# One buffer of expert rows for both expert layers, and a reordered retention with its output bias as a one-row product

## The chip, the cores and the metric

The kernel runs on one core of a Trainium2 chip. The metric is the time of one execution in device microseconds; the kernel before takes 1552.9 us, the median of three runs (1551.34 to 1556.41). The engines are TensorE (PE, with its weight loads as PEld), VectorE (DVE), ScalarE (ACT), GpSimd (POOL) and SyncE (SP, which only issues transfers).

## What is computed

The input is 4 sequences of 1024 tokens of width 256, float32. Four layers follow each other, each on the layernorm of its input and each added to it:

```
x = x + time_mix(layernorm(x))       # RWKV recurrence, projections r, k, v, output
x = x + experts(layernorm(x))        # 64 experts, 4 chosen per token, and 2 shared ones
x = x + retention(layernorm(x))      # 16 heads of 16, decay gamma, group norm, gate
x = x + experts(layernorm(x))        # the same weights again
```

The retention, cut to what matters here:

```
scores = einsum('bhnd,bhmd->bhnm', q, k) * dmask        # dmask = gamma ** (n - m)
ret    = einsum('bhnm,bhmv->bhnv', scores, v)
norm   = (ret - mean) * rsqrt(var + EPS) * gn_w + gn_b  # mean, var over a whole head of a sequence
out    = silu(x @ wg + bg) * norm @ wo + bo
```

The experts take, for each token, the four experts of highest logit plus bias, and sum their outputs with the softmax of the four logits.

## The kernel before

The 4096 tokens lie as 32 tiles of 128 in SBUF (`k.res`, 128 partitions, 32 tiles, 256 floats), where every layer adds to them. Four stages run one after the other: `time_mix`, `experts` ("moe1"), `retention`, `experts` ("moe2"). Each stage gives every engine a program of its own; engines wait for each other on semaphores, and the order of work on an engine is written out by hand.

**Experts.** In the first half tokens are routed. Each token gets four slots in a DRAM buffer of rows sorted by expert, 192 pages of 128 rows, and GpSimd scatters the normalised row to each of them (L857, 16 indirect transfers for each of 8 blocks of 4 tiles). Slots that no token takes must hold defined values, so the whole buffer is cleared before. There are two such buffers (`Slots.x`): that of moe1 has rows of 256 floats and is cleared at the end of `time_mix`'s SP program, that of moe2 has rows of 264, with a tail of 8 (the chosen experts and the numbers of the token's choices), and is cleared within the retention. Clearing is 48 transfers by `zero_slots` (L2328 to L2334), each of 512 or 528 KB. While rows are scattered, SP loads the experts' down weights over those parts of `xn` whose scatters have landed (L638, and L1091 for the last part). In the second half (`experts_*`) the pages are read in pairs (L1076), transposed (L1112), multiplied by gate and up weights (L1123), gated, multiplied by the down weights (L1136) and stored. In moe1 the stored rows are gathered only within the retention: for each tile of tokens four indirect transfers by GpSimd (L457), and VectorE adds the four with their weights (`add_pair`, L485).

**Retention** (L1490 on). Batch b is a sequence: 8 tiles, in two halves of 4. VectorE adds the choices in pairs of tiles (`add_choices(b, pair)`), takes the statistics of a half (`statistics(b, h)`), GpSimd raises the variance to the power -1/2 (`layernorm_power`, L1995), ScalarE normalises (L1889), TensorE transposes (L1714) and projects (L1730, L1735), ScalarE adds the biases and VectorE keeps the values (`keep_values`, L2133). GpSimd multiplies k and q by the decay (`decay_k`, L2004; `decay_q`, L2012), two instructions each for a half. Then the eight chunks of the batch: scores (L1777), mask on VectorE (L2143), output (L1748, L1754), update of the state (L1789; L2152, L2156). After them the group norm: sums over the group (L1798), mean, squares on ScalarE, variance (L2173), `group_power` on GpSimd (L2024), the gate on VectorE (L2181 to L2188). Then the output: four PSUM banks of two tiles, each tile two products of 128x256 (L1811), and VectorE adds each bank to `k.res` (L2211). TensorE's program for a batch is: chunks of b, first half's transposes and projections of b+1, those of the second half with the two group sums between them, output of b. `add_output_bias` (L2015 to L2020) adds the output bias to all 8 tiles of a batch on GpSimd, after ScalarE has normalised them, and VectorE's `output` waits for that.

A gather of tile t takes its place in a ring of 8 tiles and waits until the choices of tile t-8 have been added; from batch 1 on each gather also waits until the gather two before it has landed (`apart`). SP's program of the retention ends with the clearing of the second buffer: four transfers each time that another pair of tiles has been added, from the pair 4 on.

GpSimd's loop body before, for b = 0, 1, 2:

```
if b: gather(b+1, tiles 5, 6, 7)          # tiles 4 to 7 of batch 1 stand before the loop
gather(b+2, 0, 1, 2); layernorm_power(b+1, second half); gather(b+2, 3)
decay_k(b+1, first half); add_output_bias(b+1); layernorm_power(b+2, first half)
group_power(b); gather(b+2, 4); wait for the gate of b
decay_q(b+1, first); decay_k(b+1, second); decay_q(b+1, second)
```

## Time and profile before

| | |
|---|---|
| median of three runs | 1552.9 us |
| the profiled execution | 1554.35 us |
| its span, first to last instruction | 1552.7 us |
| time mixing | 0 to about 195 us |
| first expert layer | about 195 to 604 us |
| retention | about 604 to 1005 us |
| second expert layer | about 1005 us to the end |
| busy: TensorE, VectorE, GpSimd, ScalarE | 1276.3, 1110.2, 935.1, 686.9 us |
| mean granted clock of TensorE | 0.918 of full speed |
| clearing transfers | 48 of 512 KB and 48 of 528 KB, median 15.2 and 5.0 us to landing |

Times are microseconds from the start of the span. A timeline row is a run of like instructions of one engine: start, time from its start to the end of the last of them, line and operation, output and inputs, count, and in brackets the idle time of the engine before it and what ended it. A float32 product is two MATMUL instructions. Ends of matmuls are modelled, so distances between starts say more than durations. "128*128" is the part of the array that a matmul takes (rows*columns), and what follows it is the shape of its operand.

### The profile page before, as it was taken

What the parts mean: (1) busy time and instruction counts of PE and PEld (TensorE: products, weight loads), DVE (VectorE), ACT (ScalarE), POOL (GpSimd) and SP (SyncE); (2) the same over time, 40 slices, a digit from 0 to 9 for tenths busy, and PEclk for the clock granted to TensorE, in tenths of its full rate; (3) what the DMA queues carried; (4) which work ended last, traced back from release to release, by engine and by line L of the source; (5) the groups of instructions that cost most, each with busy time, mean ns of one, the idle gap of its engine ahead of it and who ended that gap; (6) DMA issues with size and microseconds to landing.
All of it is one profiled execution on the core that took longest, in us unless ns stands there. A gap on an engine that the chain in (4) does not pass through costs nothing. (4 is left out here: it accounts for less than half of the span.)

```text
span 1552.7 us, 24667 instructions
## 1 busy us (share of the span) xinstructions
PE 1276.3 (82%) x7400; PEld 872.7 (56%) x7400; DVE 1110.2 (72%) x2782; ACT 686.9 (44%) x1463; POOL 935.1 (60%) x1064
## 2 busy tenths in 40 slices
PE   6688666998799996988889899576998688888683
PEld 2244443665688884556465656453665566666442
DVE  4899888778366663538567766587776488888777
ACT  4999531221366664232415243231221477676520
POOL 2999747777555554765565522057777377777700
PEclk9799867999899997998999999868999899999987
DMA  9900073232788786432534430072323765655187
GB/s 360 419 7 0 0 294 102 100 108 93 229 257 280 261 282 217 124 138 84 218 104 163 156 122 1 8 302 105 112 102 115 213 198 193 214 185 156 41 312 258
DMA packets 115882, 257.41 MB, mean 166 GB/s; under 512 B 21895, under 2 KB 43822, under 8 KB 115252
## 3 DMA queue, kind: packets, MB, share of 16 engines
q1 hardware_dynamic: 87572, 188.32, 35.3%
q0 software_dynamic: 27648, 67.70, 12.8%
q8 instruction: 52, 0.85, 0.2%
q14 instruction: 66, 0.54, 0.1%
q10 hardware_dynamic: 544, 0.00, 0.0%
HBM read 124.56 MB, written 139.75 MB: 170 GB/s over the span
## 5 line engine op out<-in xcount | busy, mean ns | idle before, releaser
L857 POOL DMA_INDIRECT slots_x<-arena,slot x256 | 272.1, 1063 | 102.4 <-issue 74.2
L1204 POOL DMA_INDIRECT pairs_y<-arena x192 | 189.4, 986 | 79.8 <-issue 45.2
L1123 PE MATMUL moe_narrow<-arena 128*128 128x128 f32 x1536 | 209.5, 280 | 31.6 <-DVE arena L1267 31.2
L1123 PEld LDWEIGHTS moe_narrow<-arena 128*128 128x128 f32 x1536 | 188.5, 194 | 43.4 <-issue 41.6
L700 PE MATMUL moe_wide<-arena 128*128 128x512 f32 x384 | 188.2, 637 | 18.6 <-DVE arena L975 18.6
L1267 DVE TENSOR_TENSOR arena<-arena,moe_narrow 64x128 f32<-64x128 f32 x384 | 111.6, 291 | 98.7 <-ACT arena L1171 92.2
L457 POOL DMA_INDIRECT arena<-slots_y,slot x128 | 128.9, 1007 | 87.2 <-DMA arena<-slots_y,slot 51.3
L1165 ACT ACTIVATE arena<-moe_narrow 128x512 f32<-128x512 f32 x192 | 114.6, 597 | 104.6 <-PE moe_narrow L1123 57.0
L1112 PE MATMUL moe_narrow<-ident,arena 128*128 128x128 f32 x768 | 126.0, 289 | 17.3 <-DMA arena<-slots_x 17.3
L1275 DVE COPY arena<-moe_wide 128x512 f32<-128x512 f32 x192 | 128.4, 689 | 7.4 <-DMA pairs_y<-arena 2.7
L700 PEld LDWEIGHTS moe_wide<-arena 128*128 128x128 f32 x384 | 77.0, 207 | 99.5 <-issue 98.4
L485 DVE SCALAR_TENSOR_TENSOR residual<-arena,gate,residual 128x256 f32<-128x256 f32 x256 | 114.6, 519 | 24.2 <-DMA arena<-pairs_y 14.8
L1181 ACT ACTIVATE arena<-arena 64x256 f32 x288 | 118.5, 411 | 26.7 <-issue 13.6
L785 ACT ACTIVATE arena<-moe_wide 128x512 f32<-128x512 f32 x48 | 28.7, 597 | 217.0 <-PE moe_wide L700 217.0
L1136 PE MATMUL moe_wide<-arena 64*128 64x256 f32 x768 | 122.1, 415 | 3.1 <-ACT arena L1181 1.6
L1112 PEld LDWEIGHTS moe_narrow<-ident,arena 128*128 128x128 f32 x768 | 86.0, 144 | 63.9 <-issue 61.0
L1065 POOL COPY arena<-arena 128x256 f32 x192 | 70.8, 397 | 80.7 <-PE moe_narrow L1123 64.7
L711 PE MATMUL moe_narrow<-arena 128*128 128x256 f32 x384 | 92.7, 395 | 14.4 <-DVE arena L975 12.7
L1730 PE MATMUL ret_pj<-arena 128*128 128x512 f32 x192 | 91.0, 615 | 9.8 <-ACTq L1902 6.2
L711 PEld LDWEIGHTS moe_narrow<-arena 128*128 128x128 f32 x384 | 73.7, 197 | 27.1 <-DVE arena L975 14.4
L2143 DVE TENSOR_TENSOR arena<-ret_sc,arena 128x512 f32<-128x512 f32 x128 | 79.4, 682 | 10.4 <-PE ret_sc L1777 6.3
L1171 ACT ACTIVATE arena<-moe_narrow 64x256 f32<-64x256 f32 x192 | 72.1, 375 | 18.6 <-PE moe_narrow L1123 14.6
(273 smaller groups left out, 2409.1 us busy)
## 6 DMA issues: line engine op xcount, KB each, us to landing
slots_x<-arena SPq DMA_DIRECT2D x48, 528.0 KB, 5.0
arena<-slots_x SPq DMA_DIRECT2D x96, 264.0 KB, 2.9
slots_x<-arena SPq DMA_DIRECT2D x48, 512.0 KB, 15.2
arena<-slots_x SPq DMA_DIRECT2D x96, 256.0 KB, 3.6
slots_y<-arena SPq DMA_DIRECT2D x96, 256.0 KB, 3.1
arena<-w_gu SPq DMA_DIRECT2D x2, 8192.0 KB, 27.7
arena<-pairs_y SPq DMA_DIRECT2D x32, 512.0 KB, 4.7
residual<-x SPq DMA_DIRECT2D x8, 512.0 KB, 9.0
```

Of the source, the lines that this page charges most:

```text
L457: pool.indirect_dma_start(out=self.ring[:, t % self.G, i, :], in_=self.k.slots.y, out_offset=None, in_offset=bass.IndirectOffsetOnAxis(ap= ...
L485: dve.scalar_tensor_tensor(tile, self.ring[:, place + j, i, :], weight, tile, ALU.mult, ALU.add)\
L700: last = pe.matmul(bank[:, :], sgu[:, h, at:at + P], xnt[n % TRING][:, h, :], start=h == 0, stop=h == KH - 1)
L711: last = pe.matmul(down_ps[:, i, :], sht[:, (SH * n + m) % HRING, at:at + P], sd[:, m, :], start=m == 0, stop=m == SH - 1)
L857: pool.indirect_dma_start(out=x_slots, in_=xn[:, t, :], in_offset=None, out_offset=bass.IndirectOffsetOnAxis(ap=slot[:, t, i:i + 1], axis=0))\
L1112: last = pe.transpose(xt_ps[n % 2][:, (j * KH + h) * P:(j * KH + h + 1) * P], xin[:, n % XRING, j, h * P:(h + 1) * P], k.ident[:, :])
L1123: last = pe.matmul(h_ps[n % 2][:, j * P:(j + 1) * P], weights[:, n % 3, j, h, :], xt[:, n % XTRING, (j * KH + h) * P:(j * KH + h + 1) * P] ...
L1136: last = pe.matmul(y_ps[n % 2][:, j, 0:D], ht[rows, n % HTRING, j * P:(j + 1) * P], wd_pair[rows, n % HTRING, :], start=True, stop=True)
L1165: act.activation(xt[:, n % XTRING], xt_ps[n % 2][:, :], ACT.Copy).then_inc(exp_sem("xt_read"), 1)
L1181: act.activation(wd_pair[j * F:(j + 1) * F, n % HTRING, :], down_of(held[n][j]), ACT.Copy)\
L1204: pool.indirect_dma_start(out=slots.y_of, in_=ytile[:, n % YRING, j, :], in_offset=None, bounds_check=slots.pairs - 1, oob_is_err=False, o ...
L1275: dve.tensor_copy(ytile[:, n % YRING], y_ps[n % 2][:, :, 0:D]).then_inc(exp_sem("y_kept"), 1)
```

## The change

One buffer `slots_x` with rows of 264 floats serves both expert layers. It is cleared once, at the end of `time_mix`; the second clearing, in the retention, goes. In moe1 GpSimd clears the tails of the rows in SBUF with one memset, and the rows are scattered with them. In the retention the output bias becomes a third product for each tile: one row of ones (partition 0 of `one_row`) by one row of the bias, added into the bank of the output by TensorE. `add_output_bias` and its waits go. GpSimd's gathers, powers and decays stand in another order, and on VectorE the statistics of batch b+2 move behind the gate, in front of the output. The checks of the arena against `ZERO_AT` become checks against its whole size. Not shown are the signatures and the calls, which lose `zeroes` and `turn`.

```diff
@@ class Slots @@
-        self.x = [nc.dram_tensor(f"slots_x{turn}", (self.tiles * P, width + tail), F32, kind="Internal").ap()
-                  for turn, tail in ((1, 0), (2, self.TAIL))]
+        self.x = nc.dram_tensor("slots_x", (self.tiles * P, width + self.TAIL), F32, kind="Internal").ap()
@@ experts, route_gpsimd @@
             if scatters:
                 pool.iota(xn[:, :, D + K:D + 2 * K], ...)
+            else:
+                pool.memset(xn[:, :, D:W], 0.0).then_inc(sem("tables"), 1)
...
-            pool.wait_ge(k.slots_zeroed, 16 * k.ZEROINGS * (1 + scatters))
-            pool.wait_ge(sem("tables"), 2 if scatters else 1)
+            pool.wait_ge(k.slots_zeroed, 16 * k.ZEROINGS)
+            pool.wait_ge(sem("tables"), 2)
@@ retention, sync @@
-            PAIRS = NT // 2
-            for pair in range(TB // 2, PAIRS) if zeroes else ():
-                sp.wait_ge(sem("added"), 2 * choices.K * (pair + 1))
-                k.zero_slots(sp, 2, range(k.ZEROINGS * (pair - TB // 2) // (PAIRS - TB // 2),
-                                          k.ZEROINGS * (pair + 1 - TB // 2) // (PAIRS - TB // 2)))
@@ retention, tensor, output @@
                         for c in range(CH):
                             at = (2 * i + j) * P
-                            last = pe.matmul(outs[i % 2][:, j * D:(j + 1) * D], ret[:, c, at:at + P], wo[:, c, :],
-                                             start=c == 0, stop=c == CH - 1)
+                            pe.matmul(outs[i % 2][:, j * D:(j + 1) * D], ret[:, c, at:at + P], wo[:, c, :],
+                                      start=c == 0, stop=False)
+                        last = pe.matmul(outs[i % 2][:, j * D:(j + 1) * D], one_row[0:1, :], bias_o[0:1, :],
+                                         start=False, stop=True)
@@ retention, scalar, normalise @@
-                if h == H - 1:
-                    act.wait_ge(sem("xn_ready"), TB * (b + 1))
-                    act.sem_inc(sem("choices_added"), 1)
@@ retention, gpsimd @@
-            def add_output_bias(b):
...
             def constants():
...
+                pool.memset(one_row, 1.0).then_inc(sem("one_row"), 1)
...
             layernorm_power(H)
-            gather(1, [4, 5, 6, 7])
-            pool.wait_ge(sem("w_o"), 16 * LOADS)
-            add_output_bias(0)
+            gather(1, [4, 5])
             for b in range(B - 1):
                 more = b + 2 < B
-                if b:
-                    gather(b + 1, [5, 6, 7])
+                gather(b + 1, [6, 7])
                 if more:
-                    gather(b + 2, [0, 1, 2])
+                    gather(b + 2, range(4))
                 layernorm_power(H * (b + 1) + 1)
                 if more:
-                    gather(b + 2, [3])
-                decay_k(b + 1, 0)
-                add_output_bias(b + 1)
+                    gather(b + 2, [4, 5])
+                group_power(b)
+
+                pool.wait_ge(sem("gated"), CH * (b + 1))
+                for h in range(H):
+                    decay_k(b + 1, h)
+                    decay_q(b + 1, h)
                 if more:
                     layernorm_power(H * (b + 2))
-                group_power(b)
-                if more:
-                    gather(b + 2, [4])
-                pool.wait_ge(sem("gated"), CH * (b + 1))
-                decay_q(b + 1, 0)
-                decay_k(b + 1, 1)
-                decay_q(b + 1, 1)
             group_power(B - 1)
@@ retention, vector @@
             def output(b):
-                dve.wait_ge(sem("bias_added"), b + 1)
...
             keep_values(0, 0)
-            keep_values(0, 1)
             add_choices(1, 1)
             statistics(1, 0)
+            keep_values(0, 1)
...
                 if b + 2 < B:
                     add_choices(b + 2, 0)
                     add_choices(b + 2, 1)
-                    statistics(b + 2, 0)
                 variance(b)
                 gate(b)
                 keep_values(b + 1, 1)
+                if b + 2 < B:
+                    statistics(b + 2, 0)
                 output(b)
```

## Rows read from the trace of the kernel before

**Rows 1.** Busy times of one stretch: PE, PEld, DVE, ACT, POOL, clock, DMA share, GB/s

```profile
740.00:745.00 5.00, 4.60 (x11) 1.67 (x10) 3.14 (x8) 4.27 (x7) 4.57 (x2) 1.00 0.92 361
```

**Rows 2.** Timeline of DVE, batch 0: start us, busy us, instruction, idle before

```profile
688.39 0.76 DVE L2133 TENSOR_TENSOR arena<-ret_pj,arena 128x256 f32<-128x256 f32 x2 [14.06 <-PE ret_pj L1735]
...
696.83 0.27 DVE L2140 MEMSET arena<- 128x256 f32 x1 [0.55 <-DVE arena L2108]
...
725.06 4.93 DVE L2156 SCALAR_TENSOR_TENSOR arena<-arena 128x128 f32<-128x128 f32 x2
...
778.91 0.16 DVE L2181 TENSOR_TENSOR arena<-arena 128x2 f32<-128x2 f32 x1 [1.83 <-POOL arena L2024]
...
793.90 0.27 DVE L2140 MEMSET arena<- 128x256 f32 x1
```

**Rows 3.** Timeline of DVE, batches 1 and 2

```profile
862.64 0.16 DVE L2181 TENSOR_TENSOR arena<-arena 128x2 f32<-128x2 f32 x1 [1.83 <-POOL arena L2024]
...
876.73 0.27 DVE L2140 MEMSET arena<- 128x256 f32 x1
...
939.93 0.16 DVE L2181 TENSOR_TENSOR arena<-arena 128x2 f32<-128x2 f32 x1 [0.88 <-POOL arena L2024]
...
952.21 0.27 DVE L2140 MEMSET arena<- 128x256 f32 x1
```

**Rows 4.** Timeline of POOL, batches 0 to 2

```profile
698.23 1.03 POOL L457 DMA_INDIRECT arena<-slots_y,slot  x1 [0.49 <-issue]
...
726.01 3.82 POOL L2019 TENSOR_TENSOR residual<-residual,arena 128x2048 f32<-128x2048 f32 x1
...
756.12 1.22 POOL L1995 TENSOR_TENSOR arena<-arena,minus_half 128x4 f32<-128x4 f32 x1
...
788.28 2.49 POOL L2004 TENSOR_TENSOR arena<-arena 128x512 f32<-128x512 f32 x2
...
793.39 0.98 POOL L457 DMA_INDIRECT arena<-slots_y,slot  x1 [0.16 <-issue]
...
830.16 0.95 POOL L457 DMA_INDIRECT arena<-slots_y,slot  x1 [0.31 <-issue]
840.25 1.05 POOL L1995 TENSOR_TENSOR arena<-arena,minus_half 128x4 f32<-128x4 f32 x1 [9.13 <-DVEq L2110]
...
923.06 1.05 POOL L1995 TENSOR_TENSOR arena<-arena,minus_half 128x4 f32<-128x4 f32 x1 [27.44 <-DVEq L2110]
```

**Rows 5.** Timeline of PE, first output products of batches 0 to 2

```profile
783.31 3.75 PE L1811 MATMUL ret_rt<-arena 128*128 128x256 f32 x8 [4.75 <-DVE arena L2188]
...
867.03 3.75 PE L1811 MATMUL ret_rt<-arena 128*128 128x256 f32 x8 [5.69 <-DVE arena L2188]
...
944.33 1.97 PE L1811 MATMUL ret_rt<-arena 128*128 128x256 f32 x8 [0.17 <-DVE arena L2188]
946.13 1.89 PE L1811 MATMUL ret_sc<-arena 128*128 128x256 f32 x8
```

**Rows 6.** Timeline of PE in the two expert stages

```profile
418.18 1.06 PE L1123 MATMUL moe_narrow<-arena 128*128 128x128 f32 x8
419.07 0.60 PE L1112 MATMUL moe_narrow<-ident,arena 128*128 128x128 f32 x4
419.51 1.06 PE L1123 MATMUL moe_narrow<-arena 128*128 128x128 f32 x8
420.49 1.13 PE L1136 MATMUL moe_wide<-arena 64*128 64x256 f32 x8
421.56 0.66 PE L1112 MATMUL moe_narrow<-ident,arena 128*128 128x128 f32 x4
422.05 1.06 PE L1123 MATMUL moe_narrow<-arena 128*128 128x128 f32 x8
...
1228.98 0.70 PE L1136 MATMUL moe_wide<-arena 64*128 64x256 f32 x4
```

**Rows 7.** Timeline of POOL, start of the first expert stage

```profile
413.38 0.39 POOL L1226 COPY arena<-arena 64x256 f32 x1 [7.88 <-DMA arena<-w_d]
```

More of the change, by code:

```diff
@@ L1485, in _, with retention @@
                 sum_vector(dve)
-def retention(nc, k, w_qk, w_vg, w_o, b_q, b_k, b_vg, b_o, gn_w, gn_b, gamma, sw_gu, sw_d, batches, zeroes):
+def retention(nc, k, w_qk, w_vg, w_o, b_q, b_k, b_vg, b_o, gn_w, gn_b, gamma, sw_gu, sw_d, batches):
     B = batches
@@ L1526, in retention @@
     blocks = arena.take(P)
+    one_row = arena.take(P)
     stats = arena.take(BLK, 6)
@@ L2013, in decay_q @@
                         .then_inc(sem("qst_ready"), 1)
-            def add_output_bias(b):
-                pool.wait_ge(sem("choices_added"), b + 1)
-                tiles = k.res[:, bass.ds(TB * b, TB), :]
-                pool.tensor_tensor(tiles, tiles, bias_o.unsqueeze(1).to_broadcast([P, TB, D]), ALU.add)\
-                    .then_inc(sem("bias_added"), 1)
             def group_power(b):
```

15 lines of the change are left out of this document (8 added, 7 removed).

## The prediction

> **What bounds the kernel now.** The change touches three stages, so I read the trace by stage: first the timelines of the retention (604.6 to 1003.5 us of the span of 1552.7), then the start of the expert stage of the first expert layer. The retention is a loop over four batches. In its chunk part VectorE sets the pace and nothing of the change lies there, except one stall. Between the chunk parts stands a chain: layernorm power on GpSimd, ScalarE's normalisation, TensorE's transposes and projections, the group's variance, VectorE's gate, TensorE's output products, VectorE's adds, and the next chunk part, whose first VectorE instruction is the memset of L2140. Three lengths of the chain matter:
> - From power (L1995, the second half's) to the start of the gate (L2181): batch 2, where nothing else is queued, needs 923.06 to 939.93, 16.9 us. Batch 0 needs 756.12 to 778.91, 22.8, and batch 1 840.25 to 862.64, 22.4 [rows 2 to 4].
> - From the first output product (L1811) to the next L2140: 783.31 to 793.90, 10.6 us in batch 0; 867.03 to 876.73, 9.7 in batch 1; 944.33 to 952.21, 7.9 in batch 2 [rows 2, 3, 5]. The first eight matmuls are at 3.75 us in the first two and 1.97 in the third: TensorE had stood idle for 4.75 and 5.69 us before and ran at half rate, in batch 2 it had not [rows 5].
> - The power itself. In batch 1 GpSimd sat idle 9.13 us before it and waited for VectorE. In batch 0 it was still in its gathers [rows 4].
>
> **The change, part by part**, on the profiled execution (1554.35 us, 1.5 above the median of 1552.9; I apply the difference to the median).
>
> *Second clearing removed.* 48 transfers of 528 KB leave SP's queue. Nothing is queued behind them there but the end of the stage, so SP gains nothing. They shared the DMA engines with GpSimd's gathers: at 740 to 745 us the queues moved 361 GB/s, while a gather every 1.74 us of 131 KB is 75 [rows 1, 4]. The effect is in the gather rate below.
>
> *Bias off GpSimd.* Four additions of 3.82 us go. Beside the first, at 726.01, two small products of VectorE (L2156, on the chain of the chunk part) lasted 4.93 us [rows 2, 4]. That stall of at most 4.9 us is worth something only if GpSimd's gathers are not later, and they are (next), so I count nothing for it. The second addition stood in batch 1 between the power and the gate and is counted there.
>
> *GpSimd's order, batch 0.* Every instruction of the move counted: before the power of batch 0, it had 28 gathers (tiles 4 to 7 of the next batch, 0 to 2 of the one after) and a bias addition; now it has 32 (four more: tile 3) and none. The first 16 took 698.23 to 726.01, 1.74 each; the 24 of batch 1, free of clearing, 793.39 to about 831.1, 1.57 each [rows 4]. I take 1.74 for the same first 16 and 1.65, between the two, for the other 16: 27.8 + 26.4 = 54.2 us. They start about 2.0 us earlier, at 696.2, because VectorE's statistics of the next batch no longer stand behind the values of the second half: two pairs of 0.76 us and a wait between them, before which VectorE idled 14.06 us [rows 2]. The chunk part itself starts earlier by between 0 and 2 us, which the later wait for GpSimd swallows. The power comes at 750.4 instead of 756.12. Bounds: same start and 1.74 throughout gives 755.8, no gain; 1.5 throughout gives 744.
>
> *From power to gate, batches 0 and 1.* The statistics of the batch after next move from before the variance to behind the gate, and the decay of k and the bias addition, which blocked VectorE's choices, move behind the gate or go. Next late is then TensorE, which gives the 16.9 us of batch 2. For batch 1: 22.4 to 16.9, 5.5 us. For batch 0, TensorE still idles before the late normalisation, so I take 18.5 rather than 16.9: gate at 768.9 instead of 778.91, 10.0 us. Behind the power there are 8 gathers now, 13 us, before the group's power, which is needed after 16: they just fit, and if each were 0.4 us slower the group's power would be late by one or two.
>
> *Behind the gate.* TensorE's output no longer follows an idle stretch (its projections end about when the gate ends, as in batch 2), so both batches take the 7.9 us of batch 2 before the new products: 2.7 and 1.8 us less. The statistics lie beside the first two output products. The four decays (two instructions and 2.49 us each [rows 4]) run from the gate on, 10 us in all; the first is needed when the next chunk part starts, at least 7.9 us later, the second a chunk behind it. The layernorm power behind them is needed only at the third chunk. All are hidden; uncovered, the first decay would cost 2.5 us.
> Gains: batch 0, 10.0 + 2.7 = 12.7; batch 1, 5.5 + 1.8 = 7.3; together **20.0 us**. Batches 2 and 3 gain nothing.
>
> *Third products.* Two per output bank, four banks per batch, four batches: 32, all on the chain, since VectorE's add waits for each bank. A product of 256 columns is two MATMULs. Eight take 944.33 to 946.13, 1.80 us, so streaming costs 0.45 us each; rows of contraction save nothing [rows 5]. But the trace names each matmul by a part of the array: operands of 64 rows come as 64*128, and one of a single row will not come as 128*128 (inferred). What a change of part costs shows in the first layer's expert stage, where TensorE never waits. Eight L1123 among their like take 0.89 us (418.18 to 419.07), four L1112 0.44 (419.07 to 419.51). The eight 64-row L1136 cost 0.43 more busy time than four do (1.13 against 0.70), so four more cost what two of the full array would, and eight are 0.85 of work. From 419.51 to 422.05 stand eight L1123, eight L1136 and four L1112: 2.54 us, where 0.89 + 0.85 + 0.44 = 2.18 would do [rows 6]. A round trip costs **0.36 us**. Each third product stands between full ones, so each makes a round trip: 0.45 + 0.36 = 0.81 us, by 32 is 25.9; with 0.4 more for the last batch, whose output starts after an idle stretch, **26.3 us**. Bounds: 0.45 each (14.4 in all) without the round trip, 1.0 each (32.0) if it is dearer for a single row or at a lower clock.
> The Trainium skill, TensorEngine Tiling (Array Packing), Key Properties, has a rule against this change: changing the tiling mode, and not just the tile, drains TensorE. By that rule two drains stand around each third product; the trace agrees, as far as 0.36 us per round trip is one. Without it the sum would end 11.5 us lower.
>
> *Rows of 264 in the first layer.* Scatters and loads are those of the second layer now, issued at the same pace. The last load of down weights carries five experts instead of four, and GpSimd waits 7.88 us for it [rows 7]. If landing grows with bytes that is 2 us, if its start dominates nothing; I take 0.5, the low side, since a load's wait includes the rows ahead of it. The small memsets fall into idle time; the clearing of 528 instead of 512 KB ends a hundred us before it is needed.
>
> **Sum:** -20.0 + 26.3 + 0.5 = +6.8 us, 1554.35 to 1561.2 on the profiled execution, 1552.9 to **1559.7** on the median. A measurement tells about 0.3% (4.7 us) from nothing.
>
> **Rivals.**
> 1. *The third product only streams* (place: TensorE between L1811's; price 0.45). For it: TensorE could take a single row on the full array. Against it: both neighbours in rows 6. Net -20.0 + 14.8 + 0.5 = -4.7: 1548.2. It decides by the round trip's price p: net is -4.7 + 32p, so the kernel is not slower if p is under 0.15, and slower by over 0.3% only if p is over 0.29.
> 2. *The gathers run faster* once nothing shares the queues: power at 744, gate 16.9 behind it, 8 us more gain, net -1.2: 1551.7. For it: 361 GB/s at the slow gathers. Against: the first 16 were slow with almost no other traffic.
> 3. *GpSimd stays the bound* (the reordering does not do what it says): 32 gathers at 1.74 from an unchanged start, power at 755.8, 5.4 us of batch 0 lost, and a late group's power 1.5 more: net +13.7: 1566.6.
>
> **How the numbers follow.** Forecast 0.57, rival 1 0.2, rival 2 0.12, rival 3 0.11. The forecast's own spread (product 0.7 to 0.95, gains 16 to 24) is 1554 to 1566, so some of it falls within 0.3%: of 0.57 about 0.43 is slower and 0.12 the same. Rival 1 is split evenly around -0.3%, rival 2 is mostly the same, rival 3 slower. Faster 0.18, same 0.28, slower 0.54. The range reaches to rival 1 and to rival 3: 1546 to 1567; the likeliest case alone has 1554 to 1566.
>
> **What would show it.** Right: L1811-like matmuls of one row named 32*128, and banks of the output about 3.4 us apart instead of 1.80; the memset of L2140 some 14.4 us behind the first output product of batch 2, not 7.9; L2156 nowhere near 4.9 us; the power of batch 0 near 750; the gate 17 to 18.5 us behind it; 361 GB/s gone. Wrong: banks 2.6 to 2.7 us apart (rival 1), power near 744 or 756, or a new VectorE wait on the first decays at the head of a chunk part.

## The result and the profile after

Three rounds give 1578.88 us for the changed kernel (1576.27 to 1591.23, four runs) and 1552.12 for the kernel before. The ratio is 1.0183, 95% interval 1.0155 to 1.0212: slower, by 26.8 us. The forecast was 1559.7, 6.8 us slower, with a range up to 1567. The sign was right, the size was not.

The profiled execution is the slowest of the four, 1591.23 us with a span of 1589.5, at a mean granted clock of 0.898 (0.918 before); the other three took 1576.3 to 1581.3 at 0.908 to 0.912, so this trace shows some 13 us more than the others. Time mixing and both expert layers are as long as before within about a microsecond, so the retention holds the difference. From one batch's chunk part to the next (the last to the statistics of the second expert layer):

| us | batch 0 | 1 | 2 | 3 |
|---|---|---|---|---|
| before | 97.1 | 82.8 | 75.5 | 53.0 |
| after | 93.4 | 96.4 | 85.8 | 70.8 |

The forecast had batch 0 at 91, 1 at 82, 2 at 82 and 3 at 60. Line numbers moved: the chunk memset L2140 is now L2124, the output products L1811 are L1807 with the one-row products at L1809, the gate L2181 is L2165 and the output's addition is L2194. The timeline of VectorE, batch 0, which answers to [rows 2]:

```profile
769.65 0.16 DVE L2165 TENSOR_TENSOR arena<-arena 128x2 f32<-128x2 f32 x1 [0.90 <-POOL arena L2013]
...
777.38 0.35 DVE L2091 TENSOR_SCALAR arena<-arena 128x4 f32<-128x4 f32 x1
...
777.96 0.69 DVE L2194 TENSOR_TENSOR residual<-residual,ret_rt 128x512 f32<-128x512 f32 x1
780.87 0.69 DVE L2194 TENSOR_TENSOR residual<-residual,ret_sc 128x512 f32<-128x512 f32 x1 [2.23 <-PE ret_sc L1809]
784.24 0.69 DVE L2194 TENSOR_TENSOR residual<-residual,ret_rt 128x512 f32<-128x512 f32 x1 [2.68 <-PE ret_rt L1809]
787.61 0.69 DVE L2194 TENSOR_TENSOR residual<-residual,ret_sc 128x512 f32<-128x512 f32 x1 [2.69 <-PE ret_sc L1809]
788.30 0.27 DVE L2124 MEMSET arena<- 128x256 f32 x1
```

The gate starts at 769.65 (forecast 768.9) and the banks are 3.37 us apart (forecast 3.4). Up to here the forecast holds. TensorE in the same output, a third product between the full ones:

```profile
774.05 1.10 PE L1807 MATMUL ret_rt<-arena 128*128 128x256 f32 x4 [0.20 <-DVE arena L2172]
775.08 0.69 PE L1809 MATMUL ret_rt<-arena 1*128 1x256 f32 x2
775.71 1.13 PE L1807 MATMUL ret_rt<-arena 128*128 128x256 f32 x4
776.77 0.69 PE L1809 MATMUL ret_rt<-arena 1*128 1x256 f32 x2
777.39 1.13 PE L1807 MATMUL ret_sc<-arena 128*128 128x256 f32 x4
```

A tile of two full products and a third starts 1.68 us behind the last one (775.71 to 777.39), where two full ones take 0.86: a third product adds 0.82 us of TensorE's time. The trace names its part of the array "1*128". Now batch 1:

```profile
859.27 1.45 PE L1807 MATMUL ret_rt<-arena 128*128 128x256 f32 x4 [2.28 <-DVE arena L2172]
860.65 1.22 PE L1809 MATMUL ret_rt<-arena 1*128 1x256 f32 x2
861.79 2.08 PE L1807 MATMUL ret_rt<-arena 128*128 128x256 f32 x4
863.80 1.22 PE L1809 MATMUL ret_rt<-arena 1*128 1x256 f32 x2
```

From the first bank on the same instructions take nearly twice as long, to the end of the output, as they do in batch 3. The busy times by stretch (length; PE, PEld, DVE, ACT, POOL, granted clock, DMA share, GB/s), first for the outputs of batches 0 to 3, then around the start of batch 1's output, then for the chunk parts behind batches 0 and 1, each in two pieces:

```profile
773.90:788.30 14.40, 13.52 (x48) 7.76 (x48) 6.32 (x19) 0.00 (x0) 13.04 (x12) 1.00 0.04 11
859.30:884.70 25.40, 24.64 (x48) 12.85 (x48) 6.33 (x19) 0.00 (x0) 18.57 (x18) 0.51 0.14 41
956.00:970.40 14.40, 13.54 (x49) 7.76 (x48) 4.09 (x9) 0.00 (x0) 9.87 (x8) 1.00 0.00 0
1013.40:1041.20 27.80, 25.26 (x48) 13.36 (x48) 4.02 (x6) 0.92 (x2) 0.35 (x2) 0.50 0.00 0
857.00:859.90 2.90, 0.63 (x3) 0.61 (x4) 2.90 (x5) 0.00 (x0) 0.70 (x1) 1.00 0.00 0
859.90:883.90 24.00, 24.00 (x47) 12.30 (x45) 5.00 (x15) 0.00 (x0) 17.98 (x18) 0.50 0.15 44
788.30:795.00 6.70, 6.27 (x38) 4.63 (x39) 3.52 (x9) 0.77 (x2) 3.79 (x5) 0.50 0.28 80
795.00:823.70 28.70, 27.61 (x435) 21.49 (x429) 23.95 (x48) 9.15 (x42) 17.15 (x18) 1.00 0.29 82
884.70:897.40 12.70, 12.31 (x86) 9.03 (x90) 6.96 (x15) 1.71 (x7) 0.00 (x0) 0.50 0.00 0
897.40:922.80 25.40, 24.30 (x386) 18.96 (x382) 20.48 (x42) 8.21 (x39) 0.00 (x0) 1.00 0.00 0
```

```profile
835.90 1.05 POOL L1991 TENSOR_TENSOR arena<-arena,minus_half 128x4 f32<-128x4 f32 x1 [12.71 <-DVEq L2094]
...
843.60 4.47 POOL L456 DMA_INDIRECT arena<-slots_y,slot  x1 [1.07 <-DMA arena<-slots_y,slot]
...
853.14 0.94 POOL L456 DMA_INDIRECT arena<-slots_y,slot  x1 [0.83 <-DMA arena<-slots_y,slot]
854.10 0.74 POOL L2013 TENSOR_TENSOR arena<-arena,minus_half 128x2 f32<-128x2 f32 x1
```

The variance was there at 851.73, but GpSimd had the last of eight gathers to issue, one of which had taken 4.47 us while VectorE added choices. The group's power ran at 854.10, VectorE's next step waited 2.98 us for it instead of 0.90, and TensorE stood idle for 2.28 us before 859.27. That this idleness made the clock fall is not shown by this trace; the profiles of the experiments, below, speak for and against it.

### The profile page after: what moved, and what is told of

Read it like the earlier page. It is cut to its first block and busy times, and to the rows that moved or that the text cites. A ratio compares the mean times of both kernels' runs of the same rounds, so it can differ in the third digit from the quotient of the medians.

```text
span 1589.5 us, 24724 instructions
## 1 busy us (share of the span) xinstructions
PE 1325.8 (83%) x7464; PEld 890.4 (56%) x7464; DVE 1100.9 (69%) x2782; ACT 686.8 (43%) x1463; POOL 919.0 (58%) x1062
## 5 line engine op out<-in xcount | busy, mean ns | idle before, releaser
L858 POOL DMA_INDIRECT slots_x<-arena,slot x256 | 268.8, 1050 | 108.5 <-issue 74.1
L1182 ACT ACTIVATE arena<-arena 64x256 f32 x288 | 118.5, 411 | 26.8 <-issue 9.9
L484 DVE SCALAR_TENSOR_TENSOR residual<-arena,gate,residual 128x256 f32<-128x256 f32 x256 | 108.6, 503 | 26.2 <-DMA arena<-pairs_y 14.1
L1113 PEld LDWEIGHTS moe_narrow<-ident,arena 128*128 128x128 f32 x768 | 85.6, 144 | 63.3 <-issue 60.7
L710 PE MATMUL moe_narrow<-arena 128*128 128x256 f32 x384 | 93.1, 396 | 14.5 <-DVE arena L976 12.7
```

The lines of the kernel that those rows point to most:

```text
L484: dve.scalar_tensor_tensor(tile, self.ring[:, place + j, i, :], weight, tile, ALU.mult, ALU.add)\
L710: last = pe.matmul(down_ps[:, i, :], sht[:, (SH * n + m) % HRING, at:at + P], sd[:, m, :], start=m == 0, stop=m == SH - 1)
L858: pool.indirect_dma_start(out=x_slots, in_=xn[:, t, :], in_offset=None, out_offset=bass.IndirectOffsetOnAxis(ap=slot[:, t, i:i + 1], axis=0))\
L1113: last = pe.transpose(xt_ps[n % 2][:, (j * KH + h) * P:(j * KH + h + 1) * P], xin[:, n % XRING, j, h * P:(h + 1) * P], k.ident[:, :])
L1182: act.activation(wd_pair[j * F:(j + 1) * F, n % HTRING, :], down_of(held[n][j]), ACT.Copy)\
```

## Experiments

Each experiment is an edit of the changed kernel where nothing else is said; "batches" are the four lengths of the table above, read from the one profiled execution of each kernel, and lines left out of an edit are marked by dots.

**What the third products cost.** Theory: 0.82 us each by themselves, and beyond that they keep TensorE at half clock where an output meets it. Rival: the new order of the work makes the clock fall.

`a_no_third` is the changed kernel without the third products; its output lacks the output bias.

```diff
-                            pe.matmul(outs[i % 2][:, j * D:(j + 1) * D], ret[:, c, at:at + P], wo[:, c, :],
-                                      start=c == 0, stop=False)
-                        last = pe.matmul(outs[i % 2][:, j * D:(j + 1) * D], one_row[0:1, :], bias_o[0:1, :],
-                                         start=False, stop=True)
+                            last = pe.matmul(outs[i % 2][:, j * D:(j + 1) * D], ret[:, c, at:at + P], wo[:, c, :],
+                                             start=c == 0, stop=c == CH - 1)
```

> The kernel after, with the third product left out, so that the output lacks its bias. Theory 1: the one-row products cost 0.82 us each at the full clock (26.2 us for 32) and, where the output begins at the half clock, they keep it there (some 20 us more in the median, over 30 in the profiled execution). Then this takes 1530 to 1536 us, and no output runs at the half clock for more than its first bank. Rival: the lost clock comes from the new order of the engines; then only the 26 us go, 1552 us, and outputs still run at 0.5.

1543.16 us (1539.81 to 1545.04), ratio 0.9934 [0.9916, 0.9951], between the two numbers. The products cost 1578.9 - 1543.2 = 35.7 us, not 26.3. Batches last 89.9, 79.2, 75.5 and 53.6 us: no output stays at half clock. In batch 1 the clock fell 1.3 us into the output, as in the changed kernel, but rose again 3.4 us later. So the one-row products and what they do to the clock are 35.7 us together. But the rest of the change is worth 8.6 us, not 20.

`c_before_third` is the kernel before with the one-row third product in place of GpSimd's addition and its waits, and everything else as before.

```diff
-                            last = pe.matmul(outs[i % 2][:, j * D:(j + 1) * D], ret[:, c, at:at + P], wo[:, c, :],
-                                             start=c == 0, stop=c == CH - 1)
+                            pe.matmul(outs[i % 2][:, j * D:(j + 1) * D], ret[:, c, at:at + P], wo[:, c, :],
+                                      start=c == 0, stop=False)
+                        last = pe.matmul(outs[i % 2][:, j * D:(j + 1) * D], one_row[0:1, :], bias_o[0:1, :],
+                                         start=False, stop=True)
...
-            add_output_bias(0)
...
-                add_output_bias(b + 1)
```

> The kernel before, with only the bias moved: the one-row third products in, the addition on GpSimd and its waits out; order and both buffers as before. Theory 1: the outputs of batches 0, 1 and 3 begin after idle stretches of 4 to 6 us there, so all three stay at the half clock: 26 for the products, some 25 to 30 for the clock, 4 more in the chunk parts behind, less some 7 for the additions: 1595 to 1606 us. Rival, the reordering is what loses the clock: 26 - 7 only, 1571 us.

1589.02 us (1586.14 to 1601.2), ratio 1.0263 [1.0220, 1.0305]: 37 us more than the kernel before, in the old order. That is between the two numbers, because two outputs and not three are at half clock: banks are 3.37 apart in batches 0 and 2 and 6.3 in 1 and 3. In batch 1 the output began at full clock behind 1.95 us of idleness, and the clock fell 2.2 us into it and stayed down. The new order is not needed for the loss of clock.

`e_rows32` asks for 32 rows of 1/32 instead of one row:

```diff
-                        last = pe.matmul(outs[i % 2][:, j * D:(j + 1) * D], one_row[0:1, :], bias_o[0:1, :],
+                        last = pe.matmul(outs[i % 2][:, j * D:(j + 1) * D], one_row[0:32, :], bias_o[0:32, :],
...
-                pool.memset(one_row, 1.0).then_inc(sem("one_row"), 1)
+                pool.memset(one_row, 1.0 / 32).then_inc(sem("one_row"), 1)
```

> The changed kernel with its third products over 32 rows (each 1/32) instead of one. Theory (the change of array part costs 0.4 us and, in an output that starts behind an idle stretch, holds TensorE at half clock, whatever the number of rows): the names read 32*128, banks 3.4 us apart at full clock and 6.3 at half clock in batches 1 and 3, 1575 to 1583 us. Rival (a single row is what is dear, because it keeps so little of the array at work): banks 2.6 to 3.0 apart, the clock rises within the output, 1553 to 1562 us.

1576.75 us (1570.76 to 1583.72), ratio 1.0157 [1.0117, 1.0198], as the changed kernel. Its operand comes as "32*128", banks are 3.37 apart in three batches and 6.3 in batch 3. So it is not the single row that is dear. Batch 1's output stayed at full clock here and the batch lasted 84.7 us, though the group's power was as late (VectorE waited 2.95 us for it) and TensorE idle as long (2.24 us) as in the changed kernel's profile.

`b_full_third` takes all 128 rows (1/128 each):

```diff
-                        last = pe.matmul(outs[i % 2][:, j * D:(j + 1) * D], one_row[0:1, :], bias_o[0:1, :],
+                        last = pe.matmul(outs[i % 2][:, j * D:(j + 1) * D], one_row[:, :], bias_o[:, :],
...
-                pool.memset(one_row, 1.0).then_inc(sem("one_row"), 1)
+                pool.memset(one_row, 1.0 / P).then_inc(sem("one_row"), 1)
```

> The kernel after, with the third product over all 128 rows (the row of ones becomes a block of 1/128, the bias stands in all 128 partitions), so that no matmul leaves the full array. Theory 1: 0.45 us each, 14.4 in all, and the clock rises within the first bank as before the change: 1545 to 1550 us. Rival: any third product holds the clock down (more work in a slow stretch, not its shape): 1560 to 1570 us with outputs at 0.5 throughout.

1552.11 us (1548.65 to 1557.66), ratio 1.0000 [0.9984, 1.0016]: 2 us above what was expected, and 27 below the changed kernel, for the same number of products. Its TensorE timeline in batch 2:

```profile
934.88 1.10 PE L1807 MATMUL ret_rt<-arena 128*128 128x256 f32 x4 [0.16 <-DVE arena L2172]
935.82 0.59 PE L1809 MATMUL ret_rt<-arena 128*128 128x256 f32 x2
936.26 1.02 PE L1807 MATMUL ret_rt<-arena 128*128 128x256 f32 x4
937.12 0.59 PE L1809 MATMUL ret_rt<-arena 128*128 128x256 f32 x2
937.55 1.02 PE L1807 MATMUL ret_sc<-arena 128*128 128x256 f32 x4
```

A tile every 1.29 us, 0.43 for the third product. The 0.39 between 0.82 and 0.43 is the change of array part, out and back. In batch 3 the output begins at half clock behind 4.09 us of idleness, as in the changed kernel, and the clock rises 3 us into it: the batch lasts 56.5 us, where one-row products make it 70.8. Against `a_no_third` the 32 products cost 8.9 us in the median, less than 32 times 0.43 (13.8), since in batches 0 and 1 they are partly hidden by VectorE's statistics.

`k_grouped` puts a bank's two one-row products together ahead of its four full ones, half as many changes:

```diff
+                    for j in range(2):
+                        pe.matmul(outs[i % 2][:, j * D:(j + 1) * D], one_row[0:1, :], bias_o[0:1, :],
+                                  start=j == 0, stop=False, skip_group_check=True)
                     for j in range(2):
                         for c in range(CH):
...
-                        last = pe.matmul(outs[i % 2][:, j * D:(j + 1) * D], one_row[0:1, :], bias_o[0:1, :],
-                                         start=False, stop=True)
```

> The changed kernel with the two one-row products of a bank one behind the other ahead of its four full ones, so that a bank has one change of array part and back instead of two. Theory (a round trip costs 0.4 us of itself): banks at full clock 2.9 to 3.0 us apart instead of 3.37, batch 2 84.0 to 84.5 us instead of 85.8; if TensorE stays at half clock in batches 1 and 3 all the same, banks there 5.4 to 5.7 instead of 6.31, the whole 1568 to 1574 us. Rival (fewer changes let the clock rise within the output, as with 128-row products): batch 3 57 to 60 us, 1553 to 1562 us.

1563.88 us (1554.65 to 1569.45), ratio 1.0087 [1.0056, 1.0118], 15 below the changed kernel. Banks are 2.98 us apart at full clock: one round trip less is 0.39, the same number from the other side. In batch 3:

```profile
985.70 2.04 PE L1805 MATMUL ret_rt<-arena 1*128 1x256 f32 x4 [4.09 <-DVE arena L2188]
987.67 3.78 PE L1810 MATMUL ret_rt<-arena 128*128 128x256 f32 x8
991.38 2.07 PE L1805 MATMUL ret_sc<-arena 1*128 1x256 f32 x4
993.38 3.78 PE L1810 MATMUL ret_sc<-arena 128*128 128x256 f32 x8
997.09 2.07 PE L1805 MATMUL ret_rt<-arena 1*128 1x256 f32 x4
999.10 3.78 PE L1810 MATMUL ret_rt<-arena 128*128 128x256 f32 x8
1002.81 1.21 PE L1805 MATMUL ret_sc<-arena 1*128 1x256 f32 x4
1003.95 1.99 PE L1810 MATMUL ret_sc<-arena 128*128 128x256 f32 x8
```

Three banks at half clock, 5.7 us each, and the fourth at full: with half the changes it rises late instead of not at all. Batch 3 lasts 64.7 us, between the 71 and the 57 to 60 that were expected, and the whole lies between the two ranges too. Batch 2 lasts 80.3 us, not the 84 that the shorter banks alone would give: the chunk part behind it, 3.4 us at half clock in the changed kernel, is at 1.00 throughout, as are those behind batches 0 and 1.

**Batch 3 and the idle stretch.** `g_not_last` leaves the third products out of batch 3 (the bias is missing there).

```diff
-                            pe.matmul(outs[i % 2][:, j * D:(j + 1) * D], ret[:, c, at:at + P], wo[:, c, :],
-                                      start=c == 0, stop=False)
-                        last = pe.matmul(outs[i % 2][:, j * D:(j + 1) * D], one_row[0:1, :], bias_o[0:1, :],
-                                         start=False, stop=True)
+                            last = pe.matmul(outs[i % 2][:, j * D:(j + 1) * D], ret[:, c, at:at + P], wo[:, c, :],
+                                      start=c == 0, stop=last_one and c == CH - 1)
+                        if not last_one:
+                            last = pe.matmul(outs[i % 2][:, j * D:(j + 1) * D], one_row[0:1, :], bias_o[0:1, :],
+                                             start=False, stop=True)
```

> The changed kernel without third products in batch 3 alone (the output bias is missing there). Theory (eight products of 0.82 us and an output held at half clock): batch 3 comes down from 70.8 to 53.6 us, 1560 to 1565 us. Rival (only the products' own 0.82 us count and the clock is down for another reason): batch 3 64 us, 1570 to 1574 us.

1558.28 us (1553.43 to 1576.27), ratio 1.0059 [1.0026, 1.0092]. Batch 3 comes down from 70.8 to 54.1 us, 16.7 for eight products whose own price is 6.6 (0.82 each): its output begins at half clock and is at full clock 4.9 us later. The median is 20.6 below the changed kernel's, more than batch 3 explains; in this profile batch 1's output stayed at full clock (83.4 us).

`l_filler` keeps TensorE at work in the idle stretch ahead of batch 3's output:

```diff
+                    if i == 0 and last_one:
+                        for n in range(8):
+                            pe.matmul(outs[1][:, n % 2 * D:(n % 2 + 1) * D], wo[:, 0, 0:P], wo[:, n % 2, :],
+                                      start=True, stop=True)
```

> The changed kernel with eight full-array products of the output weights (3.5 us at full clock, 8 us at half; their result is overwritten) in TensorE's idle stretch ahead of batch 3's output, where it stood idle for 4.1 us. Theory (an output with one-row products keeps the clock level at which it starts, and the idle stretch ahead sets that level): batch 3's output at full clock with banks 3.4 us apart, batch 3 58 to 62 us instead of 70.8, the whole 1566 to 1573 us. Rival (the level in batch 3 does not hang on the idle stretch, or the fillers are themselves at half clock and do not lift it): banks stay 6.3 us apart, batch 3 71 to 75 us, 1577 to 1585 us.

The chip that it ran on was slower for both kernels, above all in the expert layers (before 1786.07, this one 1803.5, ratio 1.0090 [1.0051, 1.0129]), so the time itself is not comparable and the stage is read instead. TensorE in batch 3:

```profile
1080.11 5.70 PE L1804 MATMUL ret_sc<-arena 128*128 128x256 f32 x16 [0.25 <-DVE arena L2161]
1085.64 1.03 PE L1811 MATMUL ret_rt<-arena 128*128 128x256 f32 x4
1086.60 0.69 PE L1813 MATMUL ret_rt<-arena 1*128 1x256 f32 x2
1087.22 1.13 PE L1811 MATMUL ret_rt<-arena 128*128 128x256 f32 x4
```

The first row holds the fillers, which begin when TensorE has been idle for 0.25 us. The clock had already fallen, at 1077.7 in TensorE's pauses before; it rose at 1084.1, 4.0 us into the fillers. The output then runs at a clock of 1.00 with banks 3.37 apart. Batch 3 lasts 60.7 us instead of 70.8, as the theory had it. So in batch 3 full-array work ahead of an output with one-row products brings it to full clock; without, it stays at half. The level at the start does not decide it alone, as batch 1 of the changed kernel and of `c_before_third` shows.

**Batch 1 and the late group power.** `f_early_power` moves the group's power one tile of gathers forward:

```diff
-                    gather(b + 2, [4, 5])
+                    gather(b + 2, [4])
                 group_power(b)
+                if more:
+                    gather(b + 2, [5])
```

> The changed kernel with GpSimd's group power one tile (four gathers) earlier in its order. Theory (TensorE's idle stretch ahead of batch 1's output, made by the late group power, is what puts that output at half clock): gate of batch 1 no longer late, banks there 3.4 us apart, batch 1 84 to 88 us instead of 96.4, the whole 1562 to 1570 us. Rival (the clock falls in batch 1 anyway, from the chunk part behind batch 0's products): banks stay 6.3 apart, only the late gate's 2 us return, 1574 to 1580 us.

1597.78 us (1596.52 to 1597.99), ratio 1.0292 [1.0275, 1.0309]: 19 us slower than the changed kernel, which neither theory had. In batch 1 the group power did come 2.1 us sooner behind the power, TensorE was idle for only 0.18 us, and the first two banks ran at full clock. But here is VectorE, and below it GpSimd, in batch 0:

```profile
775.27 1.39 DVE L2087 BATCH_NORM_STATS2 arena<-residual 128x6 f32<-128x256 f32 x4
...
777.50 8.47 DVE L2093 TENSOR_SCALAR arena<-arena 128x4 f32<-128x4 f32 x1
786.18 0.69 DVE L2196 TENSOR_TENSOR residual<-residual,ret_rt 128x512 f32<-128x512 f32 x1
```

```profile
776.12 2.51 POOL L2000 TENSOR_TENSOR arena<-arena 128x512 f32<-128x512 f32 x2
778.57 2.49 POOL L2008 TENSOR_TENSOR arena<-arena 128x512 f32<-128x512 f32 x2
781.02 2.48 POOL L2000 TENSOR_TENSOR arena<-arena 128x512 f32<-128x512 f32 x2
783.46 2.47 POOL L2008 TENSOR_TENSOR arena<-arena 128x512 f32<-128x512 f32 x2
```

A VectorE instruction on four numbers a partition lasts 8.47 us, to the end of GpSimd's four decays. In the changed kernel the same instruction (L2091) took 0.35 at the same place in the program; its decays had begun 2.1 us earlier, at 773.98. The tile of gathers that I had put behind the group's power pushed the decays into this phase. It happened in batch 1 as well (8.74 us). TensorE idled for 6.0 us meanwhile, in both batches the clock fell, and the two banks behind took 6.3 us each. The Trainium skill, SBUF — State Buffer, Who interferes with whom, says that GpSimd and a VectorE tensor_scalar can block each other for a whole instruction, by who issues first. The trace agrees on the block. It differs on the length: this one outlasted the starts of three further pairs of GpSimd instructions (778.57, 781.02, 783.46).

`h_full_first` has the early group power too, and full-array bias products that open the bank, those of the first two banks ahead of the wait for the gate:

```diff
+                def bias(i):
+                    pe.wait_ge(sem("rt_read"), RT_TURN * b + TB + 2 + max(i, 1))
+                    for j in range(2):
+                        pe.matmul(outs[i % 2][:, j * D:(j + 1) * D], one_row[:, :], bias_o[:, :],
+                                  start=j == 0, stop=False, skip_group_check=True)
+
+                bias(0)
+                bias(1)
                 for i in range(TB // 2):
...
+                    if i >= 2:
+                        bias(i)
...
```

> The changed kernel with the bias as a full-array product (128 rows of 1/128) that opens its bank: those of the first two banks run before the wait for the gate, those of the other two before their wait for a gated half; group power one tile earlier too. Theory (the full-array products cost only their streaming, and half of them now lie in TensorE's idle time, which also shortens the idle stretch): first two banks 1.7 apart, 3.4 to 7 us per batch less than with 128-row products at the end (1552.1), 1541 to 1548 us. Rival (their cost is a lower clock elsewhere, not their place on the chain): 1549 to 1554 us.

1566.08 us (1563.64 to 1567.4), ratio 1.0088 [1.0071, 1.0106]. A miss of both numbers, for the same stall: its L2099 lasts 8.48 us in batch 0 and 8.74 in batch 1. Batches 2 and 3 last 78.5 and 54.4 us against 78.9 and 56.5 with full-array products at the end, a small gain where the stall is absent.

`j_gathers_behind` repeats the early group power without the stall: the displaced tile's gathers stand behind the decays.

```diff
+                if b:
+                    gather(b + 1, [5])
                 gather(b + 1, [6, 7])
...
-                    gather(b + 2, [4, 5])
+                    gather(b + 2, [4])
                 group_power(b)
```

> The changed kernel with one tile's gathers (four) between power and group power instead of two tiles', the other tile's behind the decays, so that the decays start with the gate as in the changed kernel. Theory (the 8.5 us stall of VectorE in the kernel with the early group power came from decays that start 2 us behind the gate; without it the early group power keeps batch 1's output at full clock): no VectorE instruction over 3 us between gate and output, gate of batch 1 about 73 us behind its chunk part's start or less, banks of batch 1 3.4 us apart, 1562 to 1572 us. Rival (the clock of batch 1's output does not hang on the late group power): banks 6.3 us apart there, 1574 to 1581 us.

1573.73 us (1566.99 to 1577.7), ratio 1.0134 [1.0098, 1.0169]. VectorE has no instruction over 3 us between gate and output, TensorE idles 0.19 us ahead of batch 1's output, its banks are 3.37 apart, and batch 1 lasts 82.8 us instead of 96.4. The median is 5 us below the changed kernel's, and it fell between the two ranges. This does not show that the late group power made the clock fall. In the profiles of six kernels TensorE was idle for 2.0 to 2.3 us ahead of batch 1's output: in three the clock fell 0.6 to 2.2 us into it (the changed kernel, `a_no_third`, `c_before_third`), in three it did not (`b_full_third`, `e_rows32`, `l_filler`). In the five with 0.2 to 0.5 us (this one, `f_early_power` in its first two banks, `g_not_last`, `k_grouped` and `i_bias_idle`, below) it did not either. The idle stretch may be a condition; it does not decide alone, and one profile of each kernel cannot tell more. It fits that the changed kernel's other three runs were 10 to 15 us faster than the profiled one, about what batch 1 loses at half clock; they have no profile.

**What the rest of the change is worth.** `d_before_onebuf` is the kernel before with the shared buffer alone:

```diff
-        self.x = [nc.dram_tensor(f"slots_x{turn}", (self.tiles * P, width + tail), F32, kind="Internal").ap()
-                  for turn, tail in ((1, 0), (2, self.TAIL))]
+        self.x = nc.dram_tensor("slots_x", (self.tiles * P, width + self.TAIL), F32, kind="Internal").ap()
...
+            else:
+                pool.memset(xn[:, :, D:W], 0.0).then_inc(sem("tables"), 1)
...
-        retention(nc, k, w_qk, w_vg, w_o, b_q, b_k, b_vg, b_o, gn_w, gn_b, gamma, sw_gu, sw_d, x.shape[0], True)
+        retention(nc, k, w_qk, w_vg, w_o, b_q, b_k, b_vg, b_o, gn_w, gn_b, gamma, sw_gu, sw_d, x.shape[0], False)
```

> The kernel before, with only the one buffer of rows of 264 cleared once. Theory 1: GpSimd's gathers of batch 0 no longer share the queues with the clearing, its power comes 3 to 6 us earlier, the first expert layer is unchanged: 1545 to 1550 us. Rival: the transfers were hidden and wider rows cost the first layer a few us: 1552 to 1556 us.

1546.98 us (1539.87 to 1551.12), ratio 0.9969 [0.9956, 0.9983]. In its profile, the fastest of ten runs (1539.87), batch 0 falls from 97.1 to 85.9 us and the others stay; the medians are 4.8 us apart. Its power comes 52.8 us behind the start of the chunk part, where it took 59.3 [rows 2, 4], with the same 28 gathers and the addition. In `a_no_third` 32 gathers stand before the power, and it takes 57.1. So up to the power of batch 0 the new order gives back 4.3 of the 6.5 us that the missing traffic saves, and over the whole batch 4.0 of 11.2; it is ahead only in batch 1 (79.2 against 82.8). Between the medians, 1543.16 and 1546.98, lie 4 us, though `d_before_onebuf`'s profile is of a run 7 us below its median, so its batch lengths flatter it.

`i_bias_idle` draws the consequence: one buffer, the new order on VectorE and of the decays, no third products, 28 gathers before the power and 4 behind it, the other 16 behind the decays, and the bias back on GpSimd, in its idle stretch ahead of the group's power. GpSimd's part:

```diff
-            gather(1, [4, 5])
             for b in range(B - 1):
                 more = b + 2 < B
-                gather(b + 1, [6, 7])
+                gather(b + 1, [4, 5, 6, 7])
                 if more:
-                    gather(b + 2, range(4))
+                    gather(b + 2, range(3))
                 layernorm_power(H * (b + 1) + 1)
                 if more:
-                    gather(b + 2, [4, 5])
+                    gather(b + 2, [3])
+                if b == 0:
+                    pool.wait_ge(sem("w_o"), 16 * LOADS)
+                add_output_bias(b)
+                if not more:
+                    add_output_bias(b + 1)
                 group_power(b)
```

> One buffer and the reordered retention, but no third product: the bias stays with GpSimd, added to a batch in the idle stretch between the next batch's power and the batch's group power (the last batch's right behind the third's), and GpSimd has 28 gathers before the power of batch 0 and 4 behind it, the other 16 of a batch behind the decays. Theory (the product and the clock it holds down are the whole loss of the change; the order pays once the power of batch 0 is not behind 32 gathers): power of batch 0 49 to 51 us behind the start of its chunk part (56.4 in the changed kernel), batches 80 to 83, 79, 75.5 and 53 us, 1531 to 1540 us. Rival (GpSimd's additions and decays now hold VectorE's small instructions, as the 8.5 us of the kernel with the early group power): a batch 4 to 8 us longer, 1543 to 1552 us.

1534.8 us (1529.61 to 1537.92), ratio 0.9888 [0.9862, 0.9915]: faster than both kernels. Its GpSimd in batch 0, whose chunk part began at 691.67:

```profile
741.16 1.06 POOL L1990 TENSOR_TENSOR arena<-arena,minus_half 128x4 f32<-128x4 f32 x1
...
748.66 3.83 POOL L2014 TENSOR_TENSOR residual<-residual,arena 128x2048 f32<-128x2048 f32 x1
758.75 0.72 POOL L2019 TENSOR_TENSOR arena<-arena,minus_half 128x2 f32<-128x2 f32 x1 [6.26 <-DVEq L2169]
763.84 2.51 POOL L1999 TENSOR_TENSOR arena<-arena 128x512 f32<-128x512 f32 x2 [4.36 <-DVE arena L2181]
```

The power is 49.5 us behind the start. The bias costs 3.83 us of GpSimd, and 6.26 us of idleness are left behind it: no one waits for it. Batches last 81.4, 78.9, 75.5 and 53.0 us.

## Why the prediction failed

Forecast and measured, from the kernels above: everything but the third products -20.0 + 0.5 against -8.6; third products +26.3 against +35.7. Each is off by 9 to 11 us to the same side, which makes the 20 us between 6.8 and 26.8. Two steps failed, then: the clock was priced too low in the term for the third products, and the gain of the new order was put too high. Rivals 1 and 2 are refuted, by banks 3.37 us apart and a power at 751.31 instead of 744. Rival 3, GpSimd as the bound of batch 0, is half right: the power came sooner than the 755.8 that it said (its own price, 32 gathers at 1.74 from 698.23, gives 753.9), but 32 gathers ahead of it cost more than I saw.

*Price of a third product at full clock: right.* 0.45 for streaming and 0.36 for the round trip were read from [rows 5, 6]; 0.43 and 0.39 were measured, the second in two ways. (That all 32 lie on the chain was not quite so: `b_full_third` hides part of its own.) The rule of the Trainium skill (TensorEngine Tiling (Array Packing), Key Properties) that I weighed agrees with the trace here, and `b_full_third` shows that it is the change of part, not the product, that is dear.

*The clock in the term for the third products: the first failing step.* It is the "0.81 us, by 32" with 0.4 for the last batch, and with it the upper bound, "1.0 each (32.0) if it is dearer for a single row or at a lower clock". I counted "0.4 more for the last batch, whose output starts after an idle stretch", because outputs before began at half clock and rose within a bank or two [rows 5]. I took this rise for granted, and the third products take it away: a bank of 6.31 us, against 3.75 for one at half clock without them [rows 5], is 1.28 a product, and all four banks stay there. Eight products cost 16.7 us in batch 3, not 6.9. That alone is 9.8 us, as much as the term is off in the median (9.4), and batch 1 costs some 12 more in a run in which its clock falls.

*Part names: a slip.* I expected "32*128"; the trace says "1*128". The price is the same for either.

*TensorE no longer idle before batch 1's output: wrong.* The forecast said that the projections end about when the gate ends, and it warned of the eight gathers behind the power: "if each were 0.4 us slower the group's power would be late by one or two". It was late by 2.1 us (a wait of 2.98 for 0.90), mostly through one gather of 4.47, and that made the idle stretch. From power to gate batch 1 took 19.0 us, not 16.9. I had priced the delay; whether it also cost the clock stays open, as said above.

*The new order in batch 0: over-estimated, the second failing step.* In absolute times the forecast was hit (power 751.31 for 750.4, gate 769.65 for 768.9, and 18.3 us between them for 18.5). That hit is luck. The 32 gathers took 56.6 us, not 54.2 (the last 16 of them 1.82 each, not 1.65), but the first of them went at 694.68 and not at 696.2. And part of the early gate is a chunk part that began 2 us earlier in this profile, and the profiles of the experiments begin theirs between 691.7 and 697.3. Against its own start, `a_no_third` gains 2.2 us up to the power, 3.5 from there to the gate and 1.5 behind it, 7.2 in all instead of 12.7. What failed is the reference point: I took 10 us from the gate's time from the start of the span, which carries what the stages ahead vary. Behind the gate the statistics were not fully covered either. Without third products the first addition waits for them until 782.01, 4.0 us behind the gate's end at 778.0 where batch 2 of the kernel before needs 2.2.

*The stall of L2156: counted at nothing.* I argued that GpSimd's gathers would swallow it. The chunk part of batch 0 fell from 39.8 to 33.4 us, and the power is bound by the gathers, as argued; so this gain is spent on the wait for GpSimd as long as 32 gathers precede the power. What I missed is the clearing: in the kernel before, the 12 gathers from 729.99 to 756.12 took 2.18 us each, while the queues moved 219 GB/s (730 to 760 us); in `d_before_onebuf`, without the clearing, the same 12 took 1.66. In its profile the stall and the slow gathers go together and batch 0 is 11.2 us shorter. I had given the clearing no term but a slightly better gather rate.

*The first expert layer: within what can be read.* Neither expert layer's length moved by more than about 1 us.

## What to carry over

Pricing a product by its own row is not enough where TensorE's clock moves: look at the clock in and ahead of its stretch, and ask whether the new instruction keeps it from rising. Here the bias was cheap as a full-array product, dear as a one-row one, and cheapest on an engine that was idle at the time. Where two orders differ by a few instructions ahead of a critical one, count from the start of the stage, not from that of the span, and check every engine that shares the phase.

## What the runs showed that I had not expected

- One-row products between full-array ones at a granted clock of 0.50 to 0.51 (1.2 GHz) kept it there for a whole output of 25 us; with 128-row products in their place it rose 3 us into the output. All five profiles in which batch 3's output has one-row or 32-row products between full ones and an idle stretch ahead show it; the one with fillers ahead (0.25 us idle) does not. With the products grouped it rose at the fourth bank.
- The effect goes on behind the output. In the seven kernels with one-row or 32-row products singly between full ones, 17 outputs ended at full clock, and behind 13 of them TensorE's clock fell to half no later than 6 us into the chunk part and stayed there for 3 to 10 us. Behind the 21 outputs of batches 0 to 2 in the seven other kernels (no third products, full-array ones, or grouped ones) it never did. In the changed kernel's profile the four chunk parts take 141.8 us, 136.2 without third products; behind batch 1, whose output ended at half clock, 12.7 of 38.1 us are at half clock. Why it falls there, with TensorE busy for 6.27 of 6.70 us behind batch 0, no run isolates.
- A VectorE instruction of 0.35 us can last 8.5 beside a row of GpSimd's decays, or not, by a 2 us shift of their start. What decides whether it is held was not tried.
